# The last layer of a four-layer decoder: two-group batches against one stream of attention units with the feed-forward set between them

## The reference, cut to what matters

```python
# x: (4, 1024, 256), ctx: (4, 77, 256)
x = x + xattn3(values=ctx, keys=ctx, queries=layernorm(x), mask)
x = x + ffn3(layernorm(x))

def xattn3(values, keys, queries, mask):            # 16 heads of 16
    energy = where(mask == 0, -1e20, einsum('nqhd,nkhd->nhqk', q, k))
    attn = softmax(energy / sqrt(256), axis=3)
    return einsum('nhql,nlhd->nqhd', attn, v).reshape(...) @ w_out.T + b_out

def act_quant(x):                                   # 8-bit rounding with a factor for each token
    scale = 127.0 / clip(max(abs(x), axis=-1), 1e-5)
    return clip(round(x * scale), -128, 127) / scale

def ffn3(x):
    h = act_quant(x) @ weight_quant(w1).T           # 256 -> 1024 channels
    h = silu(depthwise_conv1d(h, width 3, along the tokens) + conv_b)
    return act_quant(h) @ weight_quant(w2).T        # 1024 -> 256
```

## Time and profile before

| | us |
|---|---|
| median of 3 runs | 2788.45 (2787.48 to 2790.1) |
| the profiled execution | 2789.93 |
| its span | 2788.2 |
| last layer, from 2277 to the end of the span | 511 |
| busy in the span: PE, DVE, ACT, POOL | 2324.6, 1926.3, 1500.0, 1031.7 |

### The profile page before, as it was taken

The page is one execution under the profiler, slowest core; times in us unless marked ns, Lnnn a source line. Parts: engine busy times, 40 slices in busy tenths (PEclk is TensorE's granted clock), DMA queues, the critical chain, the costliest instruction groups (busy, mean ns, idle before and its releaser), DMA issues. The chain is left out here.

```text
span 2788.2 us, 43303 instructions
## 1 busy us (share of the span) xinstructions
PE 2324.6 (83%) x16184; PEld 1905.0 (68%) x16184; DVE 1926.3 (69%) x4440; ACT 1500.0 (54%) x2462; POOL 1031.7 (37%) x1011
## 2 busy tenths in 40 slices
PE   4779788887579999999984999999999967767675
PEld 2446555554367878888874999999999954554544
DVE  4698888886355667656654666676666647978777
ACT  2457776664355565655542544444455535555555
POOL 3243444433222244434444244444444433223030
PEclk9789988886789999999996999999999988988897
DMA  8600000000100001100013555655555430001000
GB/s 265 235 1 17 1 16 16 9 9 8 33 16 1 22 29 48 45 29 23 12 32 111 158 133 127 144 125 127 127 130 129 97 61 11 31 11 31 1 16 15
DMA packets 144472, 171.03 MB, mean 61 GB/s; under 512 B 16920, under 2 KB 114053, under 8 KB 144264
## 3 DMA queue, kind: packets, MB, share of 16 engines
q1 hardware_dynamic: 114360, 136.15, 14.8%
q0 software_dynamic: 29184, 31.99, 7.8%
q10 hardware_dynamic: 720, 0.12, 0.0%
HBM read 100.73 MB, written 74.32 MB: 63 GB/s over the span
## 5 line engine op out<-in xcount | busy, mean ns | idle before, releaser
L2200 POOL DMA_INDIRECT x_after_l<-rowsout,target x160 | 259.5, 1622 | 317.0 <-DVE rowsout L2328 275.6
L164 PE MATMUL SC<-Xhi,Whi 128*128 128x320 f32 x1024 | 322.5, 315 | 11.3 <-DVE HF L2371 8.3
L164 PE MATMUL SC<-Xhi,Wlo 128*128 128x320 f32 x1024 | 317.9, 310 | 0.0
L164 PE MATMUL SC<-Xlo,Whi 128*128 128x320 f32 x1024 | 317.9, 310 | 0.0
L647 POOL TENSOR_TENSOR PR<-PR,rs 128x616 f32<-128x616 f32 x128 | 163.2, 1275 | 390.1 <-DVE rs L1041 390.0
L1408 POOL TENSOR_TENSOR ff_Hlo<-ff_HF,ff_Hhi 128x512 fp32r<-128x512 f32 x108 | 143.0, 1324 | 388.0 <-ACT ff_Hhi L1541 388.0
L2298 ACT ACTIVATE SG<-SC 128x320 f32<-128x320 f32 x256 | 111.8, 437 | 237.7 <-PE SC L164 236.5
L164 PEld LDWEIGHTS SC<-Xhi,Whi 128*128 128x128 f32 x1024 | 194.0, 189 | 15.1 <-DVE HF L2371 12.2
L2336 DVE TENSOR_TENSOR Hlo<-HF,Hhi 128x320 fp32r<-128x320 f32 x256 | 130.7, 511 | 104.4 <-ACT Hhi L2286 104.4
L1810 DVE TENSOR_TENSOR ff_HF<-ff_HG,SC 128x512 f32<-128x512 f32 x112 | 76.7, 685 | 172.4 <-ACT ff_HG L1535 112.9
L164 PEld LDWEIGHTS SC<-Xlo,Whi 128*128 128x128 f32 x1024 | 194.1, 190 | 0.0
(11 more groups left out here) (502 smaller groups left out, 6876.2 us busy)
## 6 DMA issues: line engine op xcount, KB each, us to landing
expert_in<-zeros SPq DMA_DIRECT2D x4, 5440.0 KB, 35.9
rowsin<-expert_in SPq DMA_DIRECT2D x32, 680.0 KB, 4.6
first_expert<-L_wg SPq DMA_DIRECT2D x16, 512.0 KB, 5.5
first_expert<-L_wu SPq DMA_DIRECT2D x16, 512.0 KB, 6.7
first_expert<-L_wd SPq DMA_DIRECT2D x16, 512.0 KB, 7.3
Wraw<-L_wg SPq DMA_DIRECT2D x16, 512.0 KB, 5.6
Wraw<-L_wu SPq DMA_DIRECT2D x16, 512.0 KB, 6.4
Wraw<-L_wd SPq DMA_DIRECT2D x16, 512.0 KB, 7.4
```

The source lines that it names most:

```text
L164: last = nc.tensor.matmul(out, lhs[l], rhs[r], start=start and n == 0, stop=stop and n == 2)
L2200: nc.gpsimd.indirect_dma_start(x1rows[:, :], bass.IndirectOffsetOnAxis(ap=target[j % 2][:, t:t + 1], axis=0), rowsout[j % 2][:, t, :], Non ...
```

## The change

`layer_3` is rewritten around a single sequence of slots, from -8 to 87. Slot i has unit i (there are 64, `N3`), and each engine goes through the slots with an `if` for every step that has its place there. Both halves share one score buffer (`pscores` = `SC[0]`), one transpose buffer (`ptrans` = `GP[0]`), one buffer for the token steps (`mid` = `GP[1]`) and one for everything of the feed-forward's channels (`wide` = `SC[1]`). There are four `L3PR` buffers for the one stream in place of three for each half, three sets of token buffers in place of two, and three `Z` in place of two.

```diff
+BATCH = 2 * UNITS
+CONV_AT = 24
+LAST_SLOT = BATCH * (B - 1) + 39
+def half_at(slot, after):
+    n, rest = divmod(slot - after, UNITS)
+    return n if rest == 0 and 0 <= n < NH else None
+def block_at(slot, after):
+    b, h = divmod(slot - CONV_AT - after, BATCH)
+    return (b, h) if 0 <= b < B and h < NHC else None
...
+        pscores, ptrans, wide, mid = SC[0], GP[0], SC[1], GP[1]
...
+            def product_bank(b, h):
+                return SC[(h + 1) % 2] if b == B - 1 else wide
...
+                    def root(n, i, var, done):                              # POOL
+                        pool.wait_ge(var, n + 1)
+                        nc.gpsimd.tensor_scalar(LN[i]["sd"][:, :], LN[i]["mv"][:, :, 1], EPS, None, ALU.add).then_inc(raised, 1)
+                        powers.append(n)
+                        pool.wait_ge(raised, len(powers))
+                        nc.gpsimd.tensor_tensor(LN[i]["sd"][:, :], LN[i]["sd"][:, :], minus_half[:, :], ALU.pow).then_inc(done, 1)
...
+                    for i in SLOTS_3:                                       # ACT
+                        mixed = i - LAG
+                        if 0 <= mixed < N3:
+                            take_pt(mixed)
+                        if 0 <= i < N3:
+                            exponentials(i)
+                        if 0 <= mixed < N3:
+                            take_ot(mixed)
+                        at = block_at(i, 0)
+                        if at is not None:
+                            middle_tap(*at)
...
+                        at = block_at(i, 1)
+                        if at is not None and at[1] % 2:
+                            silu(at[0], at[1] - 1)
+                            silu(*at)
...
+                    def first_product(b, h):                                # PE
+                        k = NHC * b + h
+                        free = k if b < B - 1 else k - 1
+                        ...
+                            pe.wait_ge(z_ready, free)
+                        bank = product_bank(b, h)
...
+                    for i in SLOTS_3:                                       # PE
+                        mixed, following = i - LAG, i + 1
+                        if 0 <= mixed < N3:
+                            unit_transposes(mixed)
+                        if 0 <= following < N3:
+                            unit_scores(following)
+                        if 0 <= mixed < N3:
+                            unit_values(mixed)
+                        at = block_at(i, 0)
+                        if at is not None:
+                            first_product(*at)
...
-                                nc.vector.tensor_reduce(amh[:, :, i], GP[i % 2][:, :].rearrange("p (t n) -> p t n", n=P), AX, ALU.max,
-                                                        apply_absolute_value=True).then_inc(sm["tile_taken"][i % 2], 1)
+                    def maximum(b, i):                                      # DVE
+                        dve.wait_ge(s_ready, NHC * b + HALF * (i + 1))
+                        part = SL[:, i * HALF:(i + 1) * HALF, :].rearrange("p h s -> p s h")
+                        link(nc.vector.tensor_reduce(SLM[:, i, :], part, AX, ALU.max, apply_absolute_value=True))
+                        if i:
+                            tt(SLM[:, 0, :], SLM[:, 0, :], SLM[:, 1, :], ALU.max).then_inc(max_done, 1)
...
+                    for i in SLOTS_3:                                       # DVE
+                        if 0 <= i < N3:
+                            shift(i)
+                        if 0 <= i - 1 < N3:
+                            sums(i - 1)
...
+                        at = block_at(i, 0)
+                        if at is not None:
+                            outer_taps(*at)
```

More of the change, by code:

```diff
@@ L2386, in experts, with rounded_tokens_at, batch_at @@
             sa.rezero()
+BATCH = 2 * UNITS
[4 more added lines that the diff above has]
+    return n if rest == 0 and 0 <= n < NH else None
+def rounded_tokens_at(slot):
+    for g, after in ((0, 16), (1, 15)):
+        n = half_at(slot, after)
+        if n is not None and n % G == g:
+            return n
+def block_at(slot, after):
+    b, h = divmod(slot - CONV_AT - after, BATCH)
+    return (b, h) if 0 <= b < B and h < NHC else None
+def batch_at(slot, after):
+    b, rest = divmod(slot - after, BATCH)
+    return b if rest == 0 and 0 <= b < B else None
 def layer_3(L, last_in, nc, a, sbt, GP, SC, ident, identb, onesf, headof, blockhead, eps, tokno, spare, x1rows, buf, out):
@@ L2398, in two @@
             return [sb(f"{name}_{g}", shape, dt) for g in range(G)]
[L2399 to L2406, removed]
+        XN, XT, OT = two("L3XN", [P, TT, D]), two("L3XT", [P, KC, TOK]), two("L3OT", [P, KC, TOK])
@@ new lines, in factors, with integers @@
+                    def factors(b):
+                        act.wait_ge(s2_psum, b + 1)
+                        nc.scalar.activation(S2B[:, :], wide[:, :], ACT.Copy).then_inc(s2_ready, 1)
+                    def integers(b, g):
+                        tok = slice(g * TOK, (g + 1) * TOK)
+                        for i in range(2):
+                            part = slice(i * HALF, (i + 1) * HALF)
+                            act.wait_ge(rounded, 2 * (G * b + g) + i + 1)
+                            last = nc.scalar.activation(SQ[:, part, tok], SI[:, part, tok], ACT.Copy)
+                        last.then_inc(q_ready, 1)
@@ L2666, in ln_stats, with sums @@
+                    def sums(n):
+                        dve.wait_ge(probs, n + 1)
+                        r = rs[n % NPA3]
+                        link(nc.vector.reduce_sum(r[:, :], PR[n % NPA3][:, :, 0:CTX], AX))
+                        nc.vector.reciprocal(r[:, :], r[:, :]).then_inc(rsum, 1)
+                    def ln_stats(n, i, done):
                         for t in range(TT):
[L2667 removed]
+                            last = nc.vector.bn_stats(LN[i]["stats"][:, t, :], tokens(n)[:, t, :])
@@ new lines, in round_block, with add_output @@
+                    def round_block(b, g):
+                        tok = slice(g * TOK, (g + 1) * TOK)
+                        dve.wait_ge(s2_ready, b + 1)
+                        for i in range(2):
+                            part = slice(i * HALF, (i + 1) * HALF)
+                            tt(SI[:, part, tok], SL[:, part, tok], bc_at(S2B[:, tok], 1, HALF), ALU.mult).then_inc(rounded, 1)
+                    def add_output(b, g):
+                        dve.wait_ge(o_psum, G * b + g + 1)
+                        for t in range(TT):
+                            x = tokens(G * b + g)[:, t, :]
+                            last = stt(x, wide[:, t * D:(t + 1) * D], os2[:, g * TT + t:g * TT + t + 1], x, ALU.mult, ALU.add)
+                        last.then_inc(o_ready, 1)
```

655 lines of the change are left out of this document (352 added, 303 removed).

## The result

The changed kernel takes 3007.8 us (median of 4 runs, 3006.8 to 3017.6), the kernel before 2788.8 beside it: a ratio of 1.079 [1.078, 1.081], 219 us slower. The forecast was 164 us slower, 2950 us with a range to 3010.

A forecast was written before the change was run, and what follows sets the result against it. DVE was busiest before (410 of 511 us); in the change a serial circle through DVE, PE and ACT was to bound block slots. Layer 630 at full clock + 45 for the clock = 675, +164: 2950 us, range 2870 to 3010.

The forecast's parts named there:

- The slot with a block: Places 8 to 15: unit and block in series, 9.5 us against 6.1 before; 24 slots, 82 us lost.
- The maxima: DVE's 8 strided reductions of 4096 at 7.4 us each (ends 4.4 and 8.4); DVE work up 30 us.
- Roots and tables: POOL's two root instructions at 0.3 us each (bound 1.2); 24 table loads at 1.28 in place of 13, no drain.
- place 9's term: Root at place 8 ahead of a unit's product in POOL's order: next transposes and scores 0.9 us late (2.7 at 1.2 each).
- Places 0 to 7, 68: Slots with a unit and other steps, no block: 68 us at full clock against 77 before, 9 us won a batch.
- place 5: Slot in places 0 to 7, put at 2.4 + 2.1 + 4.6 + 1.7 = 10.8 us.
- The clock: PE's clock over the last layer taken as 0.80, adding 45 us; 125 if it never rose.
- The circle: In a slot with a block, waits run through DVE, PE and ACT one after another and can't run ahead: 9.5 us.
- The tail: End of the layer: slots 64 to 71, without units, 43 us; last batch's blocks to the end 73, before 60.
- full clock with a cheap maximum: Rival: PE never slowed, reductions at 4.4 us; layer 606, program 2885 us; chance 0.14.
- DVE as the bound: Rival: a slot with a block costs its DVE work, 5.0 us; layer 465, program 2742 us; chance 0.05.
- Low clock throughout: Rival: PE's clock low over the whole layer, 630 + 125, program 3034 us; chance 0.08.

The follow-up runs named there:

- e6: Changed kernel plus 14 useless matmuls ahead of the scores on TensorE, behind the wait for ScalarE's copy, in slots with a block: 3037.8 us.
- e11: Changed kernel plus 12 useless matmuls ahead of a unit's transposes on TensorE, in slots with a block and a unit: 2994.0 us.
- e1: Changed kernel with TensorE's product of a block moved ahead of the next unit's scores: 2962.6 us.
- e2: Changed kernel with TensorE's product ahead of the scores and ScalarE's middle tap ahead of its copy of the unit's result: 2935.5 us.
- e7: Kernel before, with the roots done by GpSimd alone (addition and power) in place of ScalarE's root and VectorE's reciprocal: 2801.4 us.
- e9: Changed kernel with VectorE rounding the second half (`round_block`) before it waits for the first half's second product (`add_output`): 2985.7 us.
- e12: Changed kernel with product and middle tap first, maxima by comparisons without absolute value, second half's rounding first, and 12 useless matmuls per block slot: 2884.3 us.

## Why the prediction was right, and where it was short

1. **The slot with a block: right.** Forecast 9.5 at full clock, 12.7 at low, with VectorE idle ahead of the taps. Measured 9.3 in e6 and e11 where the clock was up, 11.8 to 12.2 in the quiet slots of the changed kernel, with 6.8 to 7.1 us of wait ahead of the taps. e1 and e2, which change only the order, give back 72 us by the medians and 82 from slot 24 on, where 82 were put down for it. That this fits to the microsecond is luck: the 82 were worked out for full clock, and the two runs are at 0.75 in slots 24 to 63.
2. **The maxima: right.** 7.4 forecast from the group with the similar pattern, 7.13 measured. The Trainium skill (VectorE: DVE Perf Modes, "Mode 1× (REGULAR) — the baseline") counts odd strides as one result per cycle; the trace doesn't agree: 7.13 us strided, 4.41 contiguous.
3. **Roots and tables: the roots mis-sized.** The power operation was taken at 0.3 us and takes 1.04 (L2525); 1.2 was the other bound. With 0.23 for the addition, place 9's term is 1.6 us and not 0.9. Its place in GpSimd's order can cost more than itself, as e7 shows. The table loads are 24 of 1.283 us, as counted. In the timeline after, a load starts at 2451.99, 0.02 us after the activation ahead of it ends, and ends 0.02 us before the silu (2453.29); in the timeline of e6 above the silu starts 0.01 us after a load. The Trainium skill (ScalarE: Activation LUTs, "What ACT_TABLE_LOAD costs") gives 2.66 with the drain; no drain shows on either side of these loads.
4. **Places 0 to 7, 68: the failed step is place 5.** The sum took the second half's multiplication (4.6) to lie beside the product. In VectorE's order `add_output` of the first half stands ahead of `round_block` of the second, so the two are one after the other: 17.8 us for 10.8. e9 shows 22 us for this order over the program by the medians, 28 from slot 24 on (places 5 and 6 of four batches). It could have been read in VectorE's loop of the changed kernel.
5. **The clock: 0.80 taken, 0.71 measured.** By the forecast's own scale (+125 from 1.00 to 0.50) the 0.09 are 22 us. e11's 14 us for 0.06 over the layer is of that size. So are the 7 us between executions of the same slots 0 to 23, at 0.73 and at 0.79.
6. **The sum.** By the medians the forecast lacks 55 us (219 against 164). Place 5 is 22 of them and the clock about 22; 11 are left. This is an estimate, since place 5 has work of TensorE in it and so part of the clock. (The profiled layer, 739 us for 675, lacks 64; that execution was 10 us above the median.)

   The forecast was 2950 with 0.71 on its own range of 2905 to 3000. Measured 3007.8 lies outside that range and 2 us inside the wider one. The circle, the maxima and the sign were right by their reasons; that the sum of what was put too low stayed inside 3010 is luck.
7. **Not forecast: VectorE's small steps beside GpSimd.** 29 us more in the five groups shown. Part of it lies in waits: at place 5 the 2.06 us of L2864 run while VectorE would wait for the product in any case. e7 shows the mechanism in the kernel before with 12 us. How much of the 29 us stands on the path in the stream no run tells apart. In the first 24 slots, 123 us for the forecast's 99 at full clock, the five groups take 15.6 us where the durations of before would make 4.5; the rest of the 24 us has the low clock (0.73) beside it. The 11 us of point 6 may be these steps; that is argued, not shown. The trace of before had the sign of it: three L2694 of 0.66 to 0.67 us, against 0.16 for the others, while L2090 ran.
8. **The tail**: 141 us from slot 63 on, forecast 126 at full clock (9.5 + 43 + 73). In e9 it is 126 as well (2856.9 to 2983.1), so 15 us of it are places 5 and 6 of the last two batches, counted in point 4. The forecast was for full clock and e9 has 0.74 there, so that the two agree is in part luck.

The rivals: full clock with a cheap maximum (2885) had both of its conditions wrong, by 0.71 and 7.13. DVE as the bound (2742) never came near, since it needs both orders of e1 and e2, and even then the parts around the blocks remain. "Low clock throughout" (3034) ended nearer the profiled 3017.6 than the forecast's 2952, but not by its reason: the clock was 0.71, not 0.5, and e11, which lifts it to 0.77, wins 14 us.

The gain that the change does make, in places 0 to 7, was forecast at 9 us a batch; measured these slots take 83.4, or 76.8 with e9's order, where the forecast put 77 on the kernel before. With this clock it makes none.

## What to carry to other kernels

When two streams are woven on in-order engines, write the circle of waits down for one slot before anything else: an instruction that another engine needs early must stand ahead of those that wait for that engine. Here two such moves, free in work, were worth 72 us, and a third 22. When an edit is worth a few microseconds, compare the stretch of the timeline that it touches as well as the totals. And count the idle time that weaving creates on TensorE: here its granted clock fell from 0.86 to 0.71 over the layer, and rose again to 0.77 when idle matmuls filled part of the gaps (e11).

## What the runs showed of the hardware

- VectorE's `tensor_scalar` and `scalar_tensor_tensor` on 128x4 numbers in SBUF take 0.16 to 0.17 us alone, and up to 2.07 beside GpSimd's `tensor_tensor`. In the last layer after, 23 of them (L2847, L2848, L2849, L2862, L2864) take over 1 us, and each of the 23 ends 0.01 to 0.03 us after a GpSimd `tensor_tensor` does. One that starts 0.02 us ahead of GpSimd's (L2847 at 2374.61, GpSimd's at 2374.63) keeps its 0.16, and the next is held (L2848, 1.07). The L2864 at place 5 starts at 2568.61 and takes 2.06 us; GpSimd's instruction (L2530) runs from 2568.29 to 2570.64.
- While a GpSimd `tensor_tensor` ran, instructions with an operand in PSUM kept their durations (12 of L2827 at 0.80 us, 3 of L2883 at 1.28), as did `reciprocal` (4 of L2863 at 0.18) and the sums in SBUF (8 of L2832 at 0.78). Why only the others are held is not shown.
- A power with 4 numbers per partition takes GpSimd 1.04 us, an addition 0.23.
- A reduction of 4096 numbers to 1024 costs 7.13 us with the four numbers of each result 4 KB apart and 4.41 with neighbours.
- More work on TensorE raised the granted clock of slots 24 to 31 from 0.72 to 0.84 and won 14 us (e11). On top of the better orders it raised the layer's clock from 0.76 to 0.80 and lost 7 us (e12).
